# The product of an expert's two projections: one VectorE instruction from the PSUM bank, in place of a ScalarE copy and a GpSimd product

## The chip, the core and the metric

The kernel runs on one core of a Trainium2 chip. The metric is the device time of one execution in microseconds (us). The engines are TensorE (PE in the profile; its weight loads are PEld), VectorE (DVE), ScalarE (ACT), GpSimd (POOL) and SyncE (SP, which only issues DMAs). All data is float32.

## The reference, cut to what matters

Input x is (4, 1024, 256). It is normalised, and then goes both through a Mamba block and through a mixture of experts; the output is the sum of x and both.

```python
xn = _layernorm(x)
# Mamba block on xn: skip, x_in = two projections; conv over 4 taps, silu; delta = softplus(x @ wd1.T @ wd2.T + b)
h = exp(d_l * A) * h + (d_l * x_l) * b_l      # scan over 1024 positions, 512 channels x 16 states
y = (sum over states of h * c + x * W_D) * silu(skip);  out = resid + y @ out_w.T
# mixture of experts on xn: 8 experts, 2 for each token
h = einsum('td,edf->etf', xf, W1);  v = einsum('td,edf->etf', xf, V1)
out = einsum('etf,efd->etd', silu(h) * v, W2)   # each token weighted by its two scores
```

The change is in `silu(h) * v`.

## The kernel before, in words

The Mamba block works on chunks of 256 positions, 16 chunks (c = 0 to 15), 16 states in each (n). One step is u = 16 c + n. In each step POOL makes `ub` (products), PE transposes it into the banks `bps`, ACT makes `aexp`, DVE runs four scans `hb` (L1058) from `bps`, PE transposes `hb` into the banks `hps`, and DVE adds them up in `yac` (L1072, "the sum"). All other work is cut into pieces, which the tables `B_PLACES`, `O_PLACES` and `F_PLACES` put at 32 places of a chunk, two for each state. Every engine goes through the same list of places and does its own share of each piece, in this order: on PE `turn_products(u)`, the pieces of the even place, `turn_states(u - 1)`, the pieces of the odd place; on DVE `scans(u)`, the even place, `sum_states(u - 1)`, the odd place. Engines run their own instructions in order and wait for each other by semaphores.

Experts run in chunks 2 to 13. There are 72 tiles (j) of 128 dispatched tokens, six for each chunk, each in three pieces:

- FA(j): PE multiplies the tile by W1 into bank H (L941), ACT takes tanh (`th`), DVE makes `g1` (L1236) from `th` and bank H, which is 2 h times the sigmoid of h. PE also transposes `vs`, the product of tile j - 1, into bank G (L948).
- FB(j): PE multiplies by V1 into bank V (L963). ACT copies bank V to `vs` (L665), and POOL multiplies `vs` by `g1` in place (L775).
- FC(j + 1): PE multiplies the transposed product of tile j by W2 into bank X (L971).

The FB pieces stand at places 1, 10, 14, 20, 22 and 28 of a chunk, the FA pieces at 0, 8, 13, 16, 22 and 27.

Other pieces named below: O1, O2 and O3 finish the chunk before (O1 and O2 at place 2; in O2 DVE makes `tqO`, L1207, from bank G, which PE needs free for B1, L838, at place 5). B1 to B5 and others prepare the next chunk: X2 (DVE L1186, `x`, from two SBUF tiles, places 10 and 15), B4 at place 21 (PE writes banks H and V), SP at place 23 (two large activations on ACT, each with a table load beside it), B5 at place 29 (PE transposes `xc` into banks H and V, L882).

The banks H, V, X and G are each one PSUM bank, shared by all pieces. Two semaphores count for each: `full` (PE has written it) and `free` (the reader has done with it). `USES` holds the number of each piece's use of a bank:

```python
def wait_free(eng, b, piece):       # before a piece writes bank b
    at_least(eng, free[b], USES[b, piece])
def wait_taken(eng, b, piece):      # until this piece's use of bank b was read
    at_least(eng, free[b], USES[b, piece] + 1)
```

A semaphore `s_g` counts POOL's products; PE waits for it before it transposes `vs`, DVE before it writes `g1` again.

Of the kernel before, what the change touches and what calls it, by code (L numbers as in the profile page):

```python
# [18 lines left out]
ALU = mybir.AluOpType  # L19
ACT = mybir.ActivationFunctionType  # L20
# [175 lines left out]
def mamba_moe(nc, x, norm_w, skip_wT, in_wT, conv_w, conv_b, wd1T, wd2T, wd2_b, wBCT, A_log, W_D, out_wT,  # L196
# [3 lines left out]
    with ctx:  # L200
# [3 lines left out]
        def sem(name):  # L204
            return ctx.enter_context(nc.semaphore(name))
# [125 lines left out]
        s_th = sem("s_th")  # L331
        s_g = sem("s_g")
        y_out = [sem("y_out0"), sem("y_out1")]
# [160 lines left out]
        def _(act):  # L494
# [29 lines left out]
            def do(piece):  # L524
# [130 lines left out]
                elif kind == "FB":  # L655
                    j = piece[1]
                    if j + 1 < JT:
                        wait_full(act, "X", piece)
                        if j < 0:
                            act.wait_ge(lgt, TT)  # L660
                        nc.scalar.activation(xT[:, (j + 1) % 2, :, :], bank["X"][:, 0:D].rearrange("p (k t) -> p k t", k=KD),  # L661
                                             ACT.Copy).then_inc(free["X"], 1)
                    if j >= 0:
                        wait_full(act, "V", piece)
                        nc.scalar.activation(vs[:, :], bank["V"][:, :], ACT.Copy).then_inc(free["V"], 1)  # L665
                elif kind == "FC" and piece[1] > 0:
# [29 lines left out]
        def _(pool):  # L696
# [27 lines left out]
            def do(piece):  # L724
# [36 lines left out]
                elif kind == "D":  # L761
# [3 lines left out]
                    for t in (2 * piece[1], 2 * piece[1] + 1):  # L765
                        pool.wait_ge(xn_r, TT + t + 1)
                        for sl in (sl1, sl2):
                            nc.gpsimd.indirect_dma_start(
                                out=xbuf, out_offset=bass.IndirectOffsetOnAxis(ap=sl[:, t:t + 1], axis=0),
                                in_=ring[t % RING], in_offset=None).then_inc(disp[t % RING], 16)  # L770
                elif kind == "FB" and piece[1] >= 0:
                    j = piece[1]
                    wait_taken(pool, "V", piece)
                    wait_taken(pool, "H", ("FA", j))
                    nc.gpsimd.tensor_tensor(vs[:, :], g1[:, :], vs[:, :], ALU.mult).then_inc(s_g, 1)  # L775
                elif kind == "S":
                    t = piece[1]
                    if t == 0:
                        for k in range(2):
                            pool.wait_ge(y_out[k], 16 * JT // 2)  # L780
                    for tn in ahead(t):
                        gather(tn)
                elif kind == "LD":
                    gather(TT - 1)
# [22 lines left out]
        def _(pe):  # L807
# [22 lines left out]
            def do(piece):  # L830
# [100 lines left out]
                elif kind == "FA":  # L931
# [12 lines left out]
                    if j > 0:  # L944
                        wait_free(pe, "G", piece)
                        pe.wait_ge(s_g, j)
                        for k in range(FF // P):
# [47 lines left out]
        def _(dve):  # L995
# [170 lines left out]
            def do(piece):  # L1166
# [65 lines left out]
                elif kind == "FA" and piece[1] < JT:  # L1232
                    j = piece[1]
                    dve.wait_ge(s_th, j + 1)
                    at_least(dve, s_g, j)
                    v.scalar_tensor_tensor(out=g1[:, :], in0=th[:, :], scalar=1.0, in1=bank["H"][:, :],  # L1236
                                           op0=ALU.add, op1=ALU.mult).then_inc(free["H"], 1)
                elif kind == "S":
                    t = piece[1]
# [66 lines left out]
```

## Time and profile before

| | |
|---|---|
| device time, three runs | 1483.13 us median, 1481.66 to 1486.64 |
| profiled execution, span from first to last instruction | 1480.3 us |
| its own time beside the span | not recorded apart; the span is 1.4 us under the fastest run |
| busy: PE, DVE, ACT, POOL | 1279.1, 1243.6, 915.7, 868.9 us |
| share of the span | 86%, 84%, 62%, 59% |
| the chain that ended last | PE 65%, DVE 21%, issue 6%, ACT 3%, POOL 2% |

A share of busy time is an average over stages that differ: the router and the dispatch come up to about 260 us, the experts from there to about 1260 us, then the gathering of their results. In the rows of the trace, `x8` is a run of eight like instructions shown as one, whose first number is the start and whose second is the time from its start to its end. In square brackets stands the engine's idle time just before the run, and what ended it. The timeline counts two instructions for each of the 512 columns wide matmuls (x4 for the two of a piece).

### The profile page before, as it was taken

The numbers are of one execution on the slowest core, as the hardware profiler recorded it, in microseconds if no ns is written. First come the engines' busy times: TensorE is split into PE (matmuls) and PEld (weight loads), VectorE is DVE, ScalarE is ACT, GpSimd is POOL, SyncE is SP. The second block draws the span as 40 slices with busy tenths as digits, with TensorE's granted clock in tenths as the row PEclk, the third lists the DMA queues.
The fourth block names the chain that finished last, engine by engine and source line by source line (L and its number), as shares of the span: only waits on it lengthen the run. The fifth ranks groups of instructions, "written<-read, shape, count | busy, mean of one in ns | idle before, by whom it ended". The sixth has DMA issues, their size and how long they took to land.

```text
span 1480.3 us, 24598 instructions
## 1 busy us (share of the span) xinstructions
PE 1279.1 (86%) x7476; PEld 1028.4 (69%) x7476; DVE 1243.6 (84%) x2066; ACT 915.7 (62%) x2017; POOL 868.9 (59%) x1284
## 2 busy tenths in 40 slices
PE   4686674999999999999999999999999999865765
PEld 3575553777778777777778777777878777754654
DVE  6787876889797888889797888889797898999996
ACT  3776676576675757566675757566575756755330
POOL 0332477766668585766758585666758545335563
PEclk8797877999999999999999999999999999976876
DMA  9400826000000000001000000001000100144232
GB/s 316 144 2 0 291 97 211 17 25 24 29 23 30 29 23 22 29 23 30 26 26 30 30 22 23 26 26 30 23 29 30 30 23 15 49 133 133 74 112 84
DMA packets 76093, 86.43 MB, mean 58 GB/s; under 512 B 9920, under 2 KB 67136, under 8 KB 75968
## 3 DMA queue, kind: packets, MB, share of 16 engines
q1 hardware_dynamic: 69536, 68.02, 14.4%
q0 software_dynamic: 6144, 16.79, 3.8%
q8 instruction: 65, 1.06, 0.3%
q14 instruction: 60, 0.49, 0.1%
q10 hardware_dynamic: 288, 0.07, 0.0%
HBM read 49.46 MB, written 35.39 MB: 57 GB/s over the span
## 4 chain that ended last, share of the span: by engine, by line
PE 65%; DVE 21%; issue 6%; ACT 3%; POOL 2%; DMA 1%; DVEq 0%; POOLq 0%; SPq 0%; ACTq 0%
PE bps L818 12%; PE hps L827 11%; DVE hb L1058 9%; PE bankH L941 8%; PE bankX L971 8%; PE bankV L963 8%; PE bankG L850 3%; DVE yac L1072 3%; PE bankG L948 2%; PE bankG L860 2%; PE bankV L903 2%; PE bankG L863 2%; PE bankH L903 2%; PE bankV L850 1%; DVE tok L1255 1%
## 5 line engine op out<-in xcount | busy, mean ns | idle before, releaser
L1058 DVE TENSOR_TENSOR_SCAN hb<-aexp,carry,bps 128x256 f32<-128x256 f32 x768 | 509.8, 726 | 89.8 <-PE bps L818 71.5
L515 ACT ACTIVATE aexp<-delta,Am 128x256 f32<-128x256 f32 x1024 | 440.0, 503 | 60.9 <-DVE hb L1058 54.9
L1072 DVE SCALAR_TENSOR_TENSOR yac<-hps,BC,yac 128x512 f32<-128x512 f32 x480 | 334.7, 738 | 27.6 <-PE hps L827 27.4
L818 PE MATMUL bps<-idn,ub 128*128 128x128 f32 x2048 | 298.4, 290 | 62.7 <-DVE hb L1058 44.7
L827 PE MATMUL hps<-idn,hb 128*128 128x128 f32 x2048 | 292.1, 288 | 49.2 <-DVE yac L1072 44.7
L827 PEld LDWEIGHTS hps<-idn,hb 128*128 128x128 f32 x2048 | 250.6, 149 | 101.1 <-issue 79.0
L713 POOL TENSOR_SCALAR ub<-uT,BC 128x512 f32<-128x512 f32 x448 | 312.6, 710 | 11.8 <-ACT uT L602 10.5
L818 PEld LDWEIGHTS bps<-idn,ub 128*128 128x128 f32 x2048 | 250.3, 149 | 99.4 <-issue 59.5
L799 POOL COPY carry<-hb 128x4 f32<-128x4 f32 x256 | 55.7, 218 | 232.8 <-DVE hb L1058 231.2
L1058 DVE TENSOR_TENSOR_SCAN hb<-aexp,bps 128x256 f32<-128x256 f32 x256 | 154.6, 666 | 41.6 <-PE bps L818 37.9
L775 POOL TENSOR_TENSOR vs<-g,vs 128x512 f32<-128x512 f32 x72 | 91.9, 1276 | 166.2 <-ACT vs L665 165.3
L941 PE MATMUL bankH<-w,xT 128*128 x288 | 137.7, 600 | 2.9 <-issue 2.9
L971 PE MATMUL bankX<-w,gT 128*128 x576 | 136.2, 379 | 0.3 <-ACT xT L661 0.3
L963 PE MATMUL bankV<-v,xT 128*128 x288 | 135.5, 593 | 0.0
L971 PEld LDWEIGHTS bankX<-w,gT 128*128 128x128 f32 x576 | 106.5, 190 | 13.6 <-issue 0.7
L941 PEld LDWEIGHTS bankH<-w,xT 128*128 128x128 f32 x288 | 50.2, 191 | 41.8 <-issue 40.2
L665 ACT ACTIVATE vs<-bankV 128x512 f32<-128x512 f32 x72 | 42.9, 596 | 50.6 <-PE bankV L963 50.5
L376 POOL TENSOR_TENSOR y<-y,tqO 128x512 f32<-128x512 f32 x29 | 37.0, 1275 | 61.6 <-DVE tqO L1207 55.6
L963 PEld LDWEIGHTS bankV<-v,xT 128*128 128x128 f32 x288 | 49.1, 190 | 34.4 <-issue 34.4
L850 PE MATMUL bankG<-rnT,skw 128*128 128x256 f32 x256 | 63.8, 393 | 4.8 <-DVE tqO L1207 4.7
L649 ACT ACTIVATE th<-bankH 128x512 f32<-128x512 f32 x72 | 42.8, 595 | 39.6 <-PE bankH L941 39.6
L738 POOL TENSOR_SCALAR tap<-xin,cw 128x256 f32<-128x256 f32 x132 | 62.0, 478 | 4.3
(172 smaller groups left out, 1812.2 us busy)
## 6 DMA issues: line engine op xcount, KB each, us to landing
xbuf<-gT SPq DMA_DIRECT2D x8, 1152.0 KB, 11.0
tok<-xbuf SPq DMA_DIRECT2D x72, 128.0 KB, 2.2
ybuf<-tok SPq DMA_DIRECT2D x72, 128.0 KB, 1.7
w<-in_W SPq DMA_DIRECT2D x2, 4096.0 KB, 24.0
xch<-in_x SPq DMA_DIRECT2D x16, 256.0 KB, 2.9
w<-in_x SPq DMA_DIRECT2D x4, 1024.0 KB, 11.1
v<-in_V SPq DMA_DIRECT2D x1, 4096.0 KB, 15.9
tok<-in_x SPq DMA_DIRECT2D x32, 128.0 KB, 2.2
```

The source lines that it names most:

```text
L515: nc.scalar.activation(aexp[:, u % 2, e, :], delta[:, c % 2, e, :], ACT.Exp, scale=Am[:, e, n:n + 1]).then_inc(s_a, 1)
L713: nc.gpsimd.tensor_scalar(ub[:, u % 2, s, :], uT[:, c % 2, s, :], BC[:, c % 2, s, n:n + 1], 1.0, ALU.mult, ALU.mult).then_inc(s_ub, 1)
L738: return nc.gpsimd.tensor_scalar(dst, xin[:, e, w:w + CH], cw[:, e, w:w + 1], add, ALU.mult, ALU.mult if w else ALU.add)
L775: nc.gpsimd.tensor_tensor(vs[:, :], g1[:, :], vs[:, :], ALU.mult).then_inc(s_g, 1)
L818: mm = pe.transpose(bps[q][:, i * CH + s * P:i * CH + (s + 1) * P], ub[:, u % 2, s, e * P:(e + 1) * P], idn[:, :])
L827: mm = pe.transpose(hps[s][:, e * P:(e + 1) * P], hb[:, u % 2, e, s * P:(s + 1) * P], idn[:, :])
L850: mm = pe.matmul(bank[b][:, i * CH:(i + 1) * CH], w[:, k, e * P:(e + 1) * P], rnT[:, c % 2, k, :], start=(k == 0), stop=(k == KD - 1))
L941: mm = pe.matmul(bank["H"][:, :], xT[:, j % 2, k, :], w1[:, bass.ds(col + k * FF, FF)], start=(k == 0), stop=(k == KD - 1))
L963: mm = pe.matmul(bank["V"][:, :], xT[:, j % 2, k, :], v1[:, bass.ds(columns[j] + k * FF, FF)], start=(k == 0), stop=(k == KD - 1))
L971: mm = pe.matmul(bank["X"][:, 0:D], gT[:, k * P:(k + 1) * P], w2[:, bass.ds(columns[j] + k * D, D)], start=(k == 0), stop=(k == FF // P - 1))
L1058: v.tensor_tensor_scan(hb[:, u % 2, e, :], aexp[:, u % 2, e, :], bps[e // 2][:, (e % 2) * CH:(e % 2 + 1) * CH], first, ALU.mult, ALU.add). ...
L1072: ins = v.scalar_tensor_tensor(out=yac[:, c % 2, s, :], in0=hps[s][:, :], scalar=scale, in1=yac[:, c % 2, s, :], op0=ALU.mult, op1=ALU.add)
```

## The change

ACT's copy of bank V and POOL's product go. DVE multiplies `g1` by bank V and writes `vs`, in the same piece FB, and its end frees bank V. The semaphore `s_g` goes: PE's transposes of `vs` and DVE's next `g1` wait for the freeing of bank V instead.

```diff
@@ ScalarE, piece FB
-                    if j >= 0:
-                        wait_full(act, "V", piece)
-                        nc.scalar.activation(vs[:, :], bank["V"][:, :], ACT.Copy).then_inc(free["V"], 1)
@@ GpSimd
-                elif kind == "FB" and piece[1] >= 0:
-                    j = piece[1]
-                    wait_taken(pool, "V", piece)
-                    wait_taken(pool, "H", ("FA", j))
-                    nc.gpsimd.tensor_tensor(vs[:, :], g1[:, :], vs[:, :], ALU.mult).then_inc(s_g, 1)
@@ TensorE, piece FA
                         wait_free(pe, "G", piece)
-                        pe.wait_ge(s_g, j)
+                        wait_taken(pe, "V", ("FB", j - 1))
@@ VectorE
                     dve.wait_ge(s_th, j + 1)
-                    at_least(dve, s_g, j)
+                    if j > 0:
+                        wait_taken(dve, "V", ("FB", j - 1))
                     v.scalar_tensor_tensor(out=g1[:, :], in0=th[:, :], scalar=1.0, in1=bank["H"][:, :],
                                            op0=ALU.add, op1=ALU.mult).then_inc(free["H"], 1)
+                elif kind == "FB" and piece[1] >= 0:
+                    j = piece[1]
+                    wait_full(dve, "V", piece)
+                    wait_taken(dve, "H", ("FA", j))
+                    v.tensor_tensor(vs[:, :], g1[:, :], bank["V"][:, :], ALU.mult).then_inc(free["V"], 1)
```

DVE before, from the scans of place 24 to place 0 of the next chunk (`hb` are the scans, `yac` the sums, `g` is g1):

```order
L1058 SCALAR_TENSOR_TENSOR hb<-aexp,carry,bps 128x256 x4
L1072 SCALAR_TENSOR_TENSOR yac<-hps,BC,yac 128x512 x2
L1236 SCALAR_TENSOR_TENSOR g<-th,bankH 128x512
L1058 SCALAR_TENSOR_TENSOR hb<-aexp,carry,bps 128x256 x4
L1072 SCALAR_TENSOR_TENSOR yac<-hps,BC,yac 128x512 x2
L1058 SCALAR_TENSOR_TENSOR hb<-aexp,carry,bps 128x256 x4
```

DVE now, the same place:

```order
L1049 SCALAR_TENSOR_TENSOR hb<-aexp,carry,bps 128x256 x4
L1063 SCALAR_TENSOR_TENSOR yac<-hps,BC,yac 128x512 x2
L1228 SCALAR_TENSOR_TENSOR g<-th,bankH 128x512
L1049 SCALAR_TENSOR_TENSOR hb<-aexp,carry,bps 128x256 x4
L1234 TENSOR_TENSOR vs<-g,bankV 128x512
L1063 SCALAR_TENSOR_TENSOR yac<-hps,BC,yac 128x512 x2
```

The product (L1234) stands between the scans of place 28 and the sum. PE before, from FA at place 27 to B5 at place 29, with the semaphores that each row waits for:

```order
L948 MATMUL bankG<-idn,vs 128x128 [waits s_g,free_G]
...
L963 REGISTER_ALU [waits free_V]
L963 MATMUL bankV<-v,xT 128x512
...
L827 MATMUL hps<-idn,hb 128x128 [waits s_acc,s_scan]
...
L882 MATMUL bankH<-idn,xc 128x128 [waits free_H,uu]
...
L882 MATMUL bankV<-idn,xc 128x128 [waits free_V]
```

PE now, the same rows:

```order
L939 MATMUL bankG<-idn,vs 128x128 [waits free_V,free_G]
...
L954 REGISTER_ALU [waits free_V]
L954 MATMUL bankV<-v,xT 128x512
...
L818 MATMUL hps<-idn,hb 128x128 [waits s_acc,s_scan]
...
L873 MATMUL bankH<-idn,xc 128x128 [waits free_H,uu]
...
L873 MATMUL bankV<-idn,xc 128x128 [waits free_V]
```

PE's instructions stay in their order. The transposes of `vs` wait for `free_V` in place of `s_g`, and the `free_V` that B5 waits for is now given by DVE.

## Rows read from the trace of the kernel before

**Rows 1.** Busy time of each engine, experts' stretch of 1000 us, all windows together

```profile
sum 1000.00, PE 973.66 PEld 775.60 DVE 845.79 ACT 652.94 POOL 654.48; mean PE 81.14 PEld 64.63 DVE 70.48 ACT 54.41 POOL 54.54
```

**Rows 2.** Waits, 262 to 1262 us: total, times, longest

```profile
POOL vs L775 <- ACT vs L665: 165.3, 50, 6.6
...
PE bankG L838 <- DVE tqO L1207: 18.5, 12, 1.6
```

**Rows 3.** Groups of PE, 262 to 1262 us: busy, mean ns | idle before

```profile
L948 PE MATMUL bankG<-idn,vs 128*128 128x128 f32 x284 | 42.6, 273 | 0.0
```

**Rows 4.** Timeline, the start of chunk 6

```profile
607.14 0.66 DVE L1207 SCALAR_TENSOR_TENSOR tqO<-tqO,bankG 128x512 f32<-128x512 f32 x1
...
607.86 0.66 PE L838 MATMUL bankG<-idn,xch 128*128 128x128 f32 x4 [1.60 <-DVE tqO L1207]
```

**Rows 5.** Groups of DVE by form, and g1's own line (minimum/median/maximum)

```profile
L1144 DVE TENSOR_TENSOR v<-v,bankH 128x256 f32<-128x256 f32 x1 | 0.4, 420 | 0.0
...
L1236 DVE SCALAR_TENSOR_TENSOR g<-th,bankH x72: 652/686/690, 261.0 to 1257.1; 128x512 f32<-128x512 f32 x72
```

**Rows 6.** One line of DVE: duration ns minimum/median/maximum

```profile
L1186 DVE SCALAR_TENSOR_TENSOR x<-tqB,xc x32: 667/693/1217, 24.1 to 1318.3; 128x512 f32<-128x512 f32 x32
```

**Rows 7.** Timeline, places 27 to 30 of chunk 6

```profile
668.63 0.68 DVE L1236 SCALAR_TENSOR_TENSOR g<-th,bankH 128x512 f32<-128x512 f32 x1
...
669.23 2.66 DVE L1058 TENSOR_TENSOR_SCAN hb<-aexp,carry,bps 128x256 f32<-128x256 f32 x4
...
671.80 1.38 DVE L1072 SCALAR_TENSOR_TENSOR yac<-hps,BC,yac 128x512 f32<-128x512 f32 x2
671.82 0.60 PE L882 MATMUL bankV<-idn,xc 128*128 128x128 f32 x4
...
672.25 1.04 PE L818 MATMUL bps<-idn,ub 128*128 128x128 f32 x8
```

**Rows 8.** Timeline, places 12 to 22 of chunk 6

```profile
627.07 2.66 DVE L1058 TENSOR_TENSOR_SCAN hb<-aexp,carry,bps 128x256 f32<-128x256 f32 x4 [2.10 <-PE bps L818]
...
637.23 1.27 POOL L775 TENSOR_TENSOR vs<-g,vs 128x512 f32<-128x512 f32 x1
...
637.85 1.20 DVE L1186 SCALAR_TENSOR_TENSOR x<-tqB,xc 128x512 f32<-128x512 f32 x1 [0.94 <-ACT tqB L560]
...
650.17 1.39 DVE L1072 SCALAR_TENSOR_TENSOR yac<-hps,BC,yac 128x512 f32<-128x512 f32 x2
...
651.06 1.03 PE L873 MATMUL bankV<-dtT,wd 128*128 128x256 f32 x4
...
654.39 2.66 DVE L1058 TENSOR_TENSOR_SCAN hb<-aexp,carry,bps 128x256 f32<-128x256 f32 x4 [2.83 <-PE bps L818]
```

**Rows 9.** Timeline, places 22 to 26 of chunk 6

```profile
658.82 0.60 ACT L665 ACTIVATE vs<-bankV 128x512 f32<-128x512 f32 x1 [1.01 <-PE bankV L963]
659.26 1.41 DVE L1072 SCALAR_TENSOR_TENSOR yac<-hps,BC,yac 128x512 f32<-128x512 f32 x2 [1.50 <-PE hps L827]
...
663.16 1.38 DVE L1072 SCALAR_TENSOR_TENSOR yac<-hps,BC,yac 128x512 f32<-128x512 f32 x2
664.02 1.22 PE L827 MATMUL hps<-idn,hb 128*128 128x128 f32 x8
664.05 1.71 ACT L515 ACTIVATE aexp<-delta,Am 128x256 f32<-128x256 f32 x4
664.75 2.66 DVE L1058 TENSOR_TENSOR_SCAN hb<-aexp,carry,bps 128x256 f32<-128x256 f32 x4 [0.22 <-PE hps L827]
```

**Rows 10.** Timeline, places 1 and 2 of chunk 7

```profile
681.93 0.60 ACT L665 ACTIVATE vs<-bankV 128x512 f32<-128x512 f32 x1 [1.34 <-PE bankV L963]
...
682.47 2.66 DVE L1058 TENSOR_TENSOR_SCAN hb<-aexp,carry,bps 128x256 f32<-128x256 f32 x4 [0.94 <-PE bps L818]
```

**Rows 11.** Timeline, places 26 to 29 of chunk 12

```profile
1167.11 2.42 DVE L1058 TENSOR_TENSOR_SCAN hb<-aexp,bps 128x256 f32<-128x256 f32 x4 [0.46 <-ACT aexp L515]
...
1173.67 1.38 DVE L1072 SCALAR_TENSOR_TENSOR yac<-hps,BC,yac 128x512 f32<-128x512 f32 x2
...
1173.93 0.60 PE L882 MATMUL bankV<-idn,xc 128*128 128x128 f32 x4
```

More of the change, by code:

```diff
@@ L331, in mamba_moe @@
         s_th = sem("s_th")
-        s_g = sem("s_g")
         y_out = [sem("y_out0"), sem("y_out1")]
```

## The prediction, made before the changed kernel was run

> **What bounds the kernel now.** I read the busy times by stage, then the waits, then the timeline of one chunk, PE and DVE side by side. The product stands only in chunks 2 to 13, from 262 to 1262 us. In these 1000 us PE is busy for 973.66, DVE for 845.79, ACT and POOL for some 650 each [rows 1]. So PE is the bound there: a chunk repeats every 83.9 us, and at most 26 us in all are PE's idle time. Of these, 18.5 are the twelve times (1.6 us at most each) that PE waits for DVE's tqO at the start of a chunk [rows 2]. The long wait in the list, POOL's 165.3 us for ACT's copy of V, is a wait of an idle engine. The four transposes that consume the product, bankG from vs, were never late: no idle time before them [rows 3]. So a shorter way to vs buys nothing. What decides is (1) where DVE, which gets the work, has no slack against PE, and (2) when bank V comes free.
>
> The start of a chunk is such a place: tqO ends at 607.80, and PE goes on at 607.86 after 1.60 us of idle time [rows 4]. The hand-over from DVE to PE costs 0.06. DVE has no gap from its scans at place 2 up to there, so each delay of those scans is PE's.
>
> **Price of the new instruction.** No tensor_tensor of this width with one operand in PSUM stands in the trace. The nearest row is g1, 128x512 from bank H and an SBUF tile: 677 ns mean. At 128x256, a tensor_tensor from bank H takes 420 ns [rows 5]; it is half as wide, and so a floor. The ceiling is the longest x2 product, 1217 ns [rows 6]. I take 0.69 until the result is there, as g1 in the timeline, and 0.60 for the instruction behind it: from g1's start at 668.63 to that of the scans at 669.23 [rows 7]. That is 72 x 0.60 = 43 us more for DVE. ACT loses 72 copies of 0.60 us, POOL 72 products. Neither was bound, except as told under place 22.
>
> **Where it is covered.** There are six FB pieces in a chunk, at places 1, 10, 14, 20, 22 and 28. At place 10 the product delays a sum, and DVE then still has the idle 2.10 us before the scans of 627.07. At place 14 the idle 0.94 before x2 at 637.85 takes it. At place 20 it starts at about 650.17, where the sum stood, and 2.83 us of idle time follow at 654.39 [rows 8]. Bank V is also needed there by the next matmuls of PE, at 651.06: 650.17 + 0.69 + 0.06 = 650.92, in time by 0.14. These three cost nothing. If the cover failed, each would cost up to 0.60 x 12 = 7 us.
>
> **Place 22.** V is full at 658.82, when ACT's copy started. The product starts there, and the sum that stood at 659.26 moves to 659.42, by 0.16. From here DVE is what PE waits for: the transposes of 664.02 last 1.22 because the sum of 663.16 is still emptying their banks. They go with it, +0.16 for PE. The scans of 664.75 stood idle for 0.22. The view names PE, but the exponentials of ACT, started at 664.05, fit better [rows 9]. They sit behind a chain (copy of V, two large activations, two table loads) which begins earlier without the copy. So these scans start where DVE is ready, at 664.75 - 0.22 + 0.16 = 664.69, that is 0.06 earlier.
>
> **Place 28, the largest term.** B5 at place 29 writes bank V again. Before, ACT had emptied it. Now the product stands behind the scans of 669.23 in DVE's queue. It starts at 671.80 - 0.06 = 671.74, ends at 672.43, and PE can go on at 672.49, where before it went on at 671.82 [rows 7]: PE is now 0.67 late in all (0.16 of it already had). Behind it on DVE, the sum and the scans of the next state come 0.56 late, less than PE, so no more is added.
>
> **Place 1 of the next chunk.** V is full at 681.93 + 0.67 = 682.60; the product delays the scans to 683.20, where 682.47 stood with 0.94 us of idle time [rows 10]. So DVE enters the chain that ends at tqO 0.73 us late, and PE with it. After that chain DVE waits for PE again, and the next chunk begins afresh.
>
> **Chunks 4, 8 and 12** have shorter scans. In chunk 12 the wait for ACT was 0.46, so DVE gains 0.30 where the other chunks gain 0.06; the product at place 28 starts at about 1173.37, and V is free at 1174.12 against 1173.93 [rows 11]: 0.19, and 0.06 at place 1, make 0.25.
>
> **Sum.** 9 x 0.73 + 3 x 0.25 = 7.3 us. On the span of 1480.3 that gives 1487.6. The span is 2.8 below the median of the runs, 1483.13 (no separate time of the profiled execution is given), so I forecast 1490.4, 0.5% slower.
>
> **A rule against the trace.** When the x2 product of 637.85 took 1.20 us, POOL's product of two SBUF tiles was running; the shortest took 0.67 [rows 6, 8]. g1, with an operand in PSUM, took 652 to 690 ns in all 72 cases, whatever POOL did [rows 5]. So the new product should not be slowed by POOL. The Trainium skill (SBUF — State Buffer, Who interferes with whom) says that a DVE instruction with two SBUF inputs contends with a GpSimd instruction that reads SBUF, and one with at most one SBUF input does not. By that rule, the two trace observations agree, and 0.69 holds. The same skill (Perfetto Trace Analysis, Optimizing Scalar/DVE Operations) gives DVE about 65 ns more overhead on PSUM than on SBUF; an estimate from that page would add 0.065 at the three uncovered places, 12 x 3 x 0.065 = 2.3 us. g1's measured time already includes whatever PSUM costs, so I add nothing.
>
> **Rivals.**
> - *No change.* The wait for bank V is absent or hidden, and the remaining 0.16 + 0.06 per chunk make 2.6 us: 1485.8 or a little less. For it: all terms are tenths of a microsecond, read from modelled ends of matmuls. Against it: only one instruction lies between the scans' end and the need of V. Chance 0.22.
> - *DVE is the bound.* If the cover at places 10, 14 and 20 fails in part, up to 3 x 7 us come on top: 1491 to 1512; if every product counts in full, 43 us: 1526. Against it: DVE would be busy for 889 of 1000 us, with idle stretches of up to 2.8 us. Chance 0.10. The Trainium skill (Perfetto Trace Analysis, the same section) says that when DVE is saturated, work should go to Scalar; by that rule this change goes the wrong way, and the 43 us are its price.
> - *The product is slow.* If DVE and POOL block each other here as well, the product takes 1.22. That adds 0.53 at three places: 12 x 1.6 = 19 us, 1510. g1's 72 rows speak against it. Chance 0.03.
> - *Faster.* POOL's product no longer holds up the x2 product at place 15: 1.20 becomes 0.69, and 12 x 0.5 = 6 us come off DVE's chain: 1477. It decides only if PE waits for DVE just behind it. The waits show nearly none outside of the chunk's start (26 us of idle time, 18.5 of them for tqO), and the product of place 14 puts the 0.6 us back. Chance 0.07.
> - *The forecast*, 3 to 13 us slower, 1486 to 1496: chance 0.58.
>
> **How the numbers follow.** About 0.3%, 4.5 us, is what a measurement can tell from no change here. A tenth of the forecast's cases lie under it. Slower: 0.52 + 0.10 + 0.03 = 0.65, less a little for a mild case of the second rival: 0.64. Same: 0.06 + 0.22 less the part of it that is faster, 0.27. Faster: 0.09. The range takes the forecast and the no-change case, and cuts the long upper tail: 1482 to 1499. The forecast's own range is 1486 to 1496.
>
> **What the profile after would show.** Product: 72 rows on DVE, 0.65 to 0.70 us. PE's transposes of B5 into bank V: some 0.5 us idle before them, released by DVE's product, in nine of twelve chunks; PE idle for tqO still about 1.6. The period of a chunk: 84.6 in place of 83.9. ACT's chain before the exponentials at place 26: over half a microsecond earlier against the copy's start. x2 at place 15 under 1.2. What would make it wrong: no idle time before B5's transposes (no change), scans or sums that PE waits for between places 10 and 21 (more than forecast), or a product well over 0.7 us.

## The result and the profile after

The changed kernel took 1490.14 us (median of 12 runs, 1486.34 to 1494.57), the kernel before 1484.37 in the 12 runs beside it (1480.02 to 1487.65). The ratio is 1.004 with a 95% interval of [1.0027, 1.0054], so the change costs 5.8 us by the medians, and 4.0 to 8.0 by the interval. 1490.4 had been forecast, so the sum came out right. Its parts did not all come out, and the experiments below show which. Four of the timed runs below took 1750 to 7169 us (two with the register load moved in the changed kernel, one of the last experiment, one of the kernel before); all medians and ratios leave them out.

The span of the changed kernel's profile is 1484.4 us. From the waits of its experts' stretch (total, times, longest):

```profile
PE bankG L829 <- DVE tqO L1198: 18.5, 12, 1.6
```

PE's long wait is what it was, twelve waits of at most 1.6 us [rows 2]. The product itself has 72 rows, minimum, median and maximum 650, 676 and 690 ns. The x2 product is shown below it; its slowest row is now 901 ns where it was 1217 [rows 6]:

```profile
L1234 DVE TENSOR_TENSOR vs<-g,bankV x72: 650/676/690, 259.8 to 1263.2; 128x512 f32<-128x512 f32 x72
L1177 DVE SCALAR_TENSOR_TENSOR x<-tqB,xc x32: 667/693/901, 24.5 to 1321.9; 128x512 f32<-128x512 f32 x32
```

The groups of lines, again with busy time, mean ns and the idle time before:

```profile
L939 PE MATMUL bankG<-idn,vs 128*128 128x128 f32 x284 | 42.6, 273 | 0.0
L873 PE MATMUL bankV<-idn,xc 128*128 128x128 f32 x48 | 7.7, 283 | 1.7 <-DVE vs L1234 1.5
```

PE still never waits for the finished product (L939, as L948 in [rows 3]). The new entry is the second one: B5 waits for DVE's product to leave bank V, seven times, at most 0.3 us, in all for 1.5 us. Over twelve chunks that is far less than the forecast's half a microsecond each. The busy times of the experts' stretch, 262 to 1266 us (columns: length; then PE, PEld, DVE, ACT, POOL with their instructions; granted clock, DMA share, GB/s):

```profile
262.00:1266.00 1004.00, 975.00 (x5789) 773.90 (x5788) 879.98 (x1394) 613.63 (x1389) 561.18 (x924) 1.00 0.08 25
```

DVE has 34 us more, ACT 39 less, POOL 93 less than in [rows 1], and PE about the same in a stretch 4 us longer.

**The period.** The start of B1 (the transposes into bank G that wait 1.60 us for tqO [rows 4]) is a clean mark, once in each chunk. In the changed kernel the marks of chunks 6, 7 and 13 and the one behind chunk 13 are:

```profile
605.31 0.66 PE L829 MATMUL bankG<-idn,xch 128*128 128x128 f32 x4 [1.60 <-DVE tqO L1198]
...
689.77 0.66 PE L829 MATMUL bankG<-idn,xch 128*128 128x128 f32 x4 [1.60 <-DVE tqO L1198]
...
1194.17 0.66 PE L829 MATMUL bankG<-idn,xch 128*128 128x128 f32 x4 [1.60 <-DVE tqO L1198]
...
1282.22 0.66 PE L829 MATMUL bankG<-idn,xch 128*128 128x128 f32 x4 [1.60 <-DVE tqO L1198]
```

Chunk 6 is 689.77 - 605.31 = 84.46 us long, chunk 13 is 88.05. All twelve, as differences of such starts; chunk c runs from the B1 in it to the B1 of the next:

| chunk | 2 | 3 | 4 | 5 | 6 | 7 | 8 | 9 | 10 | 11 | 12 | 13 | sum |
|---|---|---|---|---|---|---|---|---|---|---|---|---|---|
| before | 83.91 | 83.46 | 83.52 | 83.94 | 83.93 | 83.50 | 83.54 | 83.97 | 83.98 | 83.46 | 83.50 | 84.85 | 1005.56 |
| after | 83.39 | 83.98 | 83.73 | 84.47 | 84.46 | 83.99 | 83.72 | 84.47 | 84.46 | 83.99 | 83.77 | 88.05 | 1012.48 |
| difference | -0.52 | +0.52 | +0.21 | +0.53 | +0.53 | +0.49 | +0.18 | +0.50 | +0.48 | +0.53 | +0.27 | +3.20 | +6.92 |

There are three things in this table: 0.5 us in each ordinary chunk and 0.2 in a chunk with short scans (0.73 and 0.25 forecast), a gain in chunk 2, and 3.2 us in chunk 13 that no step of the forecast had. Ahead of the first mark the profiled execution after was 3.3 us quicker (269.74 against 273.03), behind the last one 0.5 slower. Of the experts' work only the first tile's FA and FB stand ahead of it and the last tile's FC behind. The ten profiles up to the experiment on chunk 13 have the first mark anywhere from 269.74 to 274.67, in kernels that hardly differ up to there, so the 3.3 us are most likely spread between executions. They are why the two spans differ by only 4.1 us, while the runs' medians differ by 5.8.

**One ordinary chunk.** DVE and PE from place 26 of chunk 6 to place 1 of the next:

```profile
662.04 2.65 DVE L1049 TENSOR_TENSOR_SCAN hb<-aexp,carry,bps 128x256 f32<-128x256 f32 x4
...
669.08 0.66 DVE L1234 TENSOR_TENSOR vs<-g,bankV 128x512 f32<-128x512 f32 x1
669.79 0.66 PE L873 MATMUL bankV<-idn,xc 128*128 128x128 f32 x4 [0.23 <-DVE vs L1234]
...
671.02 2.66 DVE L1049 TENSOR_TENSOR_SCAN hb<-aexp,carry,bps 128x256 f32<-128x256 f32 x4
...
674.63 1.93 PE L932 MATMUL bankH<-w,xT 128*128 x4
...
679.85 0.69 DVE L1234 TENSOR_TENSOR vs<-g,bankV 128x512 f32<-128x512 f32 x1 [0.40 <-PE bankV L954]
680.45 2.65 DVE L1049 TENSOR_TENSOR_SCAN hb<-aexp,carry,bps 128x256 f32<-128x256 f32 x4
```

To set the two kernels side by side I measure from the chunk's B1 mark. That was 607.86 before [rows 4] and is 605.31 now, 2.55 us. B5's second half, into bank V, stood at 671.82 [rows 7], which would be 669.27 now; it stands at 669.79, 0.52 late. The product in front of it takes 0.66 and follows the scans without a gap; bank V is the obvious cause. But the idle time before B5 is only 0.23, and the matmul of FA at 674.63 is late as well, which B5 does not hold up directly. The next chunk's product stands at 679.85 with the scans 0.60 behind it, as forecast for place 1.

### The profile page after: what moved, and what is told of

It is laid out like the page before. It is cut to its first block, busy times and chain, and to the rows that moved or that the text cites. A ratio compares the mean times of both kernels' runs of the same rounds, so it can differ in the third digit from the quotient of the medians.

```text
span 1484.4 us, 24537 instructions
## 1 busy us (share of the span) xinstructions
PE 1280.7 (86%) x7476; PEld 1026.6 (69%) x7476; DVE 1280.1 (86%) x2138; ACT 877.4 (59%) x1945; POOL 776.9 (52%) x1212
## 3 DMA queue, kind: packets, MB, share of 16 engines
q8 instruction: 65, 1.06, 0.3%
## 4 chain that ended last, share of the span: by engine, by line
PE 61%; DVE 22%; issue 8%; ACT 5%; POOL 3%; DMA 2%; DVEq 0%; SPq 0%; ACTq 0%; POOLq 0%
PE bps L809 11%; PE hps L818 10%; DVE hb L1049 9%; PE bankH L932 8%; PE bankX L962 8%; PE bankV L954 7%; PE bankG L841 3%; DVE yac L1063 3%; PE bankG L939 2%; POOL xbuf L764 2%; PE bankG L851 2%; ACT aexp L514 2%; PE bankV L894 2%; PE bankG L854 1%; PE bankV L841 1%
## 5 line engine op out<-in xcount | busy, mean ns | idle before, releaser
L790 POOL COPY carry<-hb 128x4 f32<-128x4 f32 x256 | 50.8, 199 | 404.9 <-DVE hb L1049 402.8
L1228 DVE SCALAR_TENSOR_TENSOR g<-th,bankH 128x512 f32<-128x512 f32 x72 | 49.1, 681 | 19.6 <-ACT th L648 19.0
L610 ACT ACTIVATE tqO<-bankG 128x512 f32<-128x512 f32 x31 | 18.5, 598 | 80.2 <-PE bankG L841 80.2
```

The costliest lines, as they stand in the source:

```text
L790: nc.gpsimd.tensor_copy(carry[:, n, :], hb[:, u % 2, :, CH - 1]).then_inc(s_cc, 1)
```

## The experiments

Chunk 6 stands for the ordinary chunks in all of them. Single runs of one kernel spread over some 8 us, so they say little at this size; the periods say more, for they repeat: chunks 5, 6, 9 and 10 lie within 0.05 us of each other in the kernel before, and within 0.01 in the changed one (the widest are 0.17 with B5 in bank G and 0.15 with place 22 alone, so in those two a tenth of a microsecond says little). The medians of the kernel before were 1482.15 (7 runs) beside the first four kernels, 1483.73 (25 runs) beside the next four, and 1492.64 (20 runs) beside the last four. Those ran on another chip, where the first B1 stands at 280 to 282 us and not at 270 to 275; they are read by ratio and period.

**Which of the six places costs.** Three kernels make the product on DVE at some places and with ACT's copy and POOL's product at the others:

```
def by_pool(j):                      # False: DVE makes it
    return j % 6 in BY_POOL
BY_POOL = (0, 1, 2, 3, 4)            # e_dve28: place 28 on DVE alone
BY_POOL = (0, 1, 2, 3, 5)            # e_dve22: place 22
BY_POOL = (0, 4, 5)                  # e_dve_covered: places 10, 14, 20
```

*Place 28 alone.*

> Only the products of place 28 (12 of 72) are made by VectorE from bank V; the other 60 go by ScalarE's copy and GpSimd as before. My account: at place 28 the product stands behind the scans and holds bank V until B5 needs it, so the period of an ordinary chunk (start of B1 to start of B1) goes from 83.94 to 84.4 or 84.5, nearly all of the 0.53 that the whole change costs, and TensorE is idle before B5's transposes into bank V, released by VectorE's product. Rival, VectorE's load spread evenly: a sixth of 0.53, 84.03.

1489.64 us in one run; the period of chunk 6 is 84.57, just above the 84.4 to 84.5 expected. Twelve of the 72 products cost all that the 72 cost (+0.64 against +0.53), so a load spread over all places is refuted. The wait in the list of the experts' stretch, and then DVE and PE at place 29 (the lines of this kernel are numbered otherwise: L1260 is the product, L899 is B5):

```profile
PE bankV L899 <- DVE vs L1260: 5.6, 11, 0.8
```

```profile
672.14 0.66 DVE L1260 TENSOR_TENSOR vs<-g,bankV 128x512 f32<-128x512 f32 x1
...
672.85 0.66 PE L899 MATMUL bankV<-idn,xc 128*128 128x128 f32 x4 [0.54 <-DVE vs L1260]
```

Here the idle time is the half microsecond that the prediction named: without the product of place 22, B5's first half comes in time, and its second half waits visibly. In the full change the first half is itself later, and the product earlier, so the wait shows as 0.23.

These rows also say why place 28 costs more alone (0.64) than all six together (0.53). The B1 mark of this kernel is at 608.21, so the product starts 63.93 behind it, and B5's second half stands at 64.64, 0.68 late against the kernel before (63.96): almost exactly the 0.67 forecast. In the full change the product starts at 669.08 - 605.31 = 63.77, 0.16 sooner. There ACT has no copy at place 22, its exponentials come earlier, and DVE's scans with them; that takes 0.16 back at place 28. The places don't add up: with place 28 on DVE, the other five together are a gain in the ordinary chunks.

*Place 22 alone.*

> Only the products of place 22 are made by VectorE. My account: the sum behind it and TensorE with it are 0.16 later, and the scans of place 26 start 0.14 earlier as ScalarE's chain lacks the copy; the period of an ordinary chunk becomes 84.05 to 84.1. Rival, load spread evenly: 84.03. Second rival, ScalarE's missing copy is a gain in itself: under 83.9. The relative place of the scans at place 26 tells my account from the rivals.

1482.75 us in one run; the period is 84.05, +0.12 (+0.1 to 0.15 expected). The sums and scans behind the product:

```profile
660.93 1.38 DVE L1089 SCALAR_TENSOR_TENSOR yac<-hps,BC,yac 128x512 f32<-128x512 f32 x2
...
662.23 2.65 DVE L1075 TENSOR_TENSOR_SCAN hb<-aexp,carry,bps 128x256 f32<-128x256 f32 x4
```

Sums to scans is 1.30 us. It was 664.75 - 663.16 = 1.59 with 0.22 of idle time [rows 9]. So the idle time is gone. ACT's exponentials start at 660.05 here and at 659.87 in the full change, 54.64 and 54.56 behind the B1 marks, where they stood 56.19 behind: 1.6 us earlier, the copy's 0.6 and the 1.01 of idle time in front of it [rows 9]. PE's transposes into `hps`, which the view names as the releaser, come later and not earlier (56.39 against 56.16 behind the marks), which leaves the exponentials as what the scans had waited for, as the prediction supposed. DVE takes back 0.07 more of the 0.16 than I had counted.

*The three covered places.*

> The products of places 10, 14 and 20 (36 of 72) are made by VectorE, the other 36 as before. My account: they are covered, so the period of an ordinary chunk stays at 83.94 to within 0.05, with the idle time of VectorE before the scans of place 12 and of place 22 shorter by 0.6; only chunk 13, where VectorE also makes the next chunk's convolution, is longer, by 1 to 3 us. Rival, load spread evenly: half of 0.53, 84.2 in every ordinary chunk.

1484.82 us in one run. Ordinary chunks have 83.90 to 83.98 us, unchanged: covered, as forecast. Chunk 13 is 1.26 us longer, and chunk 2 is 1.09 shorter. The second looks like the fourth rival of the prediction (POOL's product no longer slows the x2 product), but most of it is another thing. Before, in chunk 2:

```profile
289.33 1.27 POOL L775 TENSOR_TENSOR vs<-g,vs 128x512 f32<-128x512 f32 x1
...
302.34 0.63 ACT L560 ACTIVATE tqB<-xc 128x512 f32<-128x512 f32 x1 [2.71 <-POOL xc L750]
...
303.00 1.21 DVE L1186 SCALAR_TENSOR_TENSOR x<-tqB,xc 128x512 f32<-128x512 f32 x1 [2.03 <-ACT tqB L560]
...
306.84 0.66 PE L818 MATMUL bps<-idn,ub 128*128 128x128 f32 x4 [0.54 <-DVE hb L1058]
```

and with the products of places 10, 14 and 20 on DVE (L1203 is x2):

```profile
300.90 0.64 ACT L577 ACTIVATE tqB<-xc 128x512 f32<-128x512 f32 x1 [2.43 <-POOL xc L767]
301.57 0.77 DVE L1203 SCALAR_TENSOR_TENSOR x<-tqB,xc 128x512 f32<-128x512 f32 x1 [0.25 <-ACT tqB L577]
```

The x2 product waited for `tqB` from ACT, ACT for the convolution `xc` from POOL, and in POOL's queue the product of place 10 (1.27 us, at 289.33) stood ahead of that convolution. PE waited 0.54 for the scans behind x2. Without POOL's products, `tqB` and x2 start 1.16 and 1.15 us sooner against the B1 marks of chunk 2 (273.03 and 272.75), and x2 takes 0.77 in place of 1.21. The shorter x2 is 0.44 us, less than half of the gain of 1.09; the earlier convolution covers it alone. In chunk 6 x2 waits 0.94 for its input and not 2.03 [rows 8], and PE does not wait behind it.

**How place 28 reaches PE.** The prediction says: by bank V. B5 has another bank to go to:

```
-    "B5": ["H", "V"]   ...  for s, b in enumerate("HV"):
+    "B5": ["H", "G"]   ...  for s, b in enumerate("HG"):
```

> The changed kernel, with the second half of B5 in bank G in place of bank V; all products on VectorE. My account: the wait for bank V at place 29 is gone, TensorE is 0.16 late from place 22 and VectorE some 0.2 to 0.3 at the end of a chunk, so the period of an ordinary chunk is 84.15 to 84.25 in place of 84.46, and the kernel 2 to 4 us faster than the changed one. Rival, VectorE's queue is the bound there with or without the bank: 84.46 stays.

1488.05 us (4 runs), ratio to before 1.0051 [1.0034, 1.0068]; the period is 84.40 (84.57 in chunk 5). This is a miss: the wait that I took for the carrier is gone, and the cost stays. B5's second half (now into bank G) no longer waits for DVE's product, and yet:

```profile
669.58 0.66 DVE L1234 TENSOR_TENSOR vs<-g,bankV 128x512 f32<-128x512 f32 x1
669.90 0.60 PE L873 MATMUL bankG<-idn,xc 128*128 128x128 f32 x4
...
671.48 2.65 DVE L1049 TENSOR_TENSOR_SCAN hb<-aexp,carry,bps 128x256 f32<-128x256 f32 x4
673.84 1.04 PE L809 MATMUL bps<-idn,ub 128*128 128x128 f32 x8
675.03 1.98 PE L932 MATMUL bankH<-w,xT 128*128 x4 [0.16 <-issue]
```

Between the transposes into bps, which end at 674.88, and FA's matmul there is a short idle time with the releaser "issue": PE waits for nothing in the profile. In the kernel before this matmul stands 0.9 us behind the end of the DVE work that PE waits for, at two places of the chunk (scans end 675.75, matmul 676.66; sum ends 664.54, matmul 665.44), and here too (674.13, 675.03). By the program, the scans (at place 27 the sum) are what PE's queue last waits for before FA. What stands between is a load into PE's registers, the column of the expert's weights, `te` (L936 of the kernel before; PEldq is the queue of the weight loads, the numbers are minimum, median, maximum):

```profile
L936 PEldq TENSOR_LOAD <-te x72: 296/301/489, 256.2 to 1253.0; - x72
L936 PEldq FUSED_REGOPS  x72: 151/151/165, 256.7 to 1253.5; - x72
```

My reading: it is a second way for a late DVE to reach PE. The wait holds back the load, and the load the matmul, while the transposes ahead of it run out. That can be tried by loading the next tile's column at the end of FB, ahead of the wait:

```
 FA:  -    col = pe.value_load(te[0:1, j:j + 1], min_val=0, max_val=(EXPERTS - 1) * WE)
      +    col = columns[j]          # (for j == 0 it is loaded here)
 FB:  +    if j + 1 < JT:
      +        columns[j + 1] = pe.value_load(te[0:1, j + 1:j + 2], min_val=0, max_val=(EXPERTS - 1) * WE)
```

*Both ways closed.*

> The changed kernel with B5's second half in bank G, and with TensorE's register load of the expert's column for tile j + 1 moved from the start of FA(j + 1) to the end of FB(j), ahead of the waits for VectorE. My new account: at the end of a chunk VectorE's lateness reaches TensorE by two ways side by side, the wait for bank V and the register load, which starts only when TensorE's wait for the last scan is over and costs 0.9 us; each alone holds TensorE back by the same 0.4 to 0.5, so only both removed show a gain. The period of an ordinary chunk is 84.0 to 84.1 in place of 84.46, the kernel some 4 to 5 us faster than the changed one. Rival, VectorE's queue is the bound without TensorE's waits: 84.4 or more stays.

1483.26 us, ratio 0.9994 [0.998, 1.0007]; the period is 83.98, as expected. The matmul now follows the transposes with no idle time:

```profile
674.31 1.04 PE L809 MATMUL bps<-idn,ub 128*128 128x128 f32 x8
675.18 1.88 PE L932 MATMUL bankH<-w,xT 128*128 x4
```

*The register load alone.*

> The changed kernel with only the register load moved; B5 stays in bank V. My new account: the matmuls of FA at place 27 start 0.4 earlier, but the wait of B5 for bank V then holds TensorE at the same time as before, so the period of an ordinary chunk stays at 84.4 to 84.46. If the register load alone was the way by which the cost came, it is 84.0 to 84.1.

1488.17 us, ratio 1.003 [1.002, 1.0041]; the period is 84.41, as expected. Now it is bank V that shows, with the wait that the prediction had in its text (L1236 is the product):

```profile
674.49 0.66 PE L873 MATMUL bankV<-idn,xc 128*128 128x128 f32 x4 [0.68 <-DVE vs L1236]
```

The four periods of chunk 6 side by side: 84.46 as changed, 84.40 without the wait for bank V, 84.41 without the register load behind the wait, 83.98 without both. Of the 0.48 us that the two edits give together, each alone gives at most 0.06: the two ways stand side by side and carry the same lateness. No single edit would have shown this. It does not follow that these 0.48 us are the cost of the change, for the register load costs in the kernel before too, as the next run shows.

*The register load in the kernel before.*

> The kernel before, with only the register load moved. My new account: both FA starts that follow a wait for VectorE (places 27 and 0) come 0.3 to 0.4 earlier, not added up, so the period of an ordinary chunk goes from 83.94 to about 83.55, and the kernel is 4 to 5 us faster than before, 0.3%. Rival, the idle time before these matmuls is covered by VectorE's chain at the start of the chunk: 83.9 stays.

1475.93 us (4 runs), ratio 0.9948 [0.9931, 0.9965]; the period is 83.56 (83.93 before, 83.55 expected). In the kernel before, the load was not covered either. It is faster than both kernels. FA's matmuls before and with the load moved:

```profile
L941 PE MATMUL bankH<-w,xT 128*128 x284 | 135.5, 600 | 2.9 <-issue 2.9
```

```profile
L941 PE MATMUL bankH<-w,xT 128*128 x284 | 133.6, 593 | 0.0
```

The idle time of 2.9 us and 1.9 us of busy time are gone; over the twelve chunks it gains 1005.56 - 1000.97 = 4.6.

Compared like with like, a third way is left. With the load moved, the kernel before has 83.56, the changed one 84.41, and the changed one without the wait for bank V 83.98. So bank V carries 0.43, and 0.42 of the cost is there with both ways closed (if B5's other bank costs the kernel before nothing, which was not tried). First the kernel before with the load moved (its B1 mark is at 603.56), then the changed one with both edits (606.29), the sum of place 28 and PE's transposes of `hb`:

```profile
667.56 1.38 DVE L1074 SCALAR_TENSOR_TENSOR yac<-hps,BC,yac 128x512 f32<-128x512 f32 x2
668.43 0.63 PE L827 MATMUL hps<-idn,hb 128*128 128x128 f32 x4
```

```profile
670.63 1.40 DVE L1065 SCALAR_TENSOR_TENSOR yac<-hps,BC,yac 128x512 f32<-128x512 f32 x2
671.52 0.63 PE L818 MATMUL hps<-idn,hb 128*128 128x128 f32 x4
```

Against the marks the sum is 0.34 late, since the product stands in front of it, and the transposes, which need the bank that the sum empties, are 0.36 late. The FA matmul is 0.35 late (672.10 against 675.18), and the next B1 0.42. This third way was read from the rows; no edit closed it.

**Chunk 13.** In this chunk DVE also makes the convolution of chunk 14 (DVE_CONV), in the changed kernel as before. PE in its places 10 to 18, in the changed kernel:

```profile
1214.03 1.22 PE L818 MATMUL hps<-idn,hb 128*128 128x128 f32 x8 [0.36 <-DVE yac L1063]
...
1230.37 0.63 PE L809 MATMUL bps<-idn,ub 128*128 128x128 f32 x4 [1.33 <-DVE hb L1049]
1231.56 0.66 PE L809 MATMUL bps<-idn,ub 128*128 128x128 f32 x4 [0.56 <-DVE hb L1049]
1232.05 3.51 PE L851 MATMUL bankG<-x,wd 128*128 128x256 f32 x8
```

and the same matmuls in the kernel before:

```profile
1213.17 1.22 PE L827 MATMUL hps<-idn,hb 128*128 128x128 f32 x8
...
1228.92 0.63 PE L818 MATMUL bps<-idn,ub 128*128 128x128 f32 x4 [1.32 <-DVE hb L1058]
1230.10 0.66 PE L818 MATMUL bps<-idn,ub 128*128 128x128 f32 x4 [0.56 <-DVE hb L1058]
1230.60 1.89 PE L860 MATMUL bankG<-x,wd 128*128 128x256 f32 x8
```

Against the B1 marks (1194.17 and 1193.74) the first row is 0.43 us late: DVE is behind with a sum, and the product of place 10 stands in front of it. The transposes into bps are 1.02 late: 1230.37 - 1194.17 = 36.20 against 35.18. So the two products cost 1.0 us here. The waits of 1.33 and 0.56 themselves are old: DVE was late with these scans before the change too. The third part is in the last row. Eight matmuls take 3.51 us where they took 1.89, 1.62 more. The stretch of the waits and the one behind it, in the changed kernel, and then in the kernel before, each moved to the same matmuls (columns as above):

```profile
1229.00:1232.00 3.00, 1.11 (x9) 0.87 (x9) 3.00 (x5) 2.74 (x6) 0.44 (x2) 1.00 0.11 37
1232.00:1235.30 3.30, 3.30 (x10) 2.64 (x9) 3.30 (x7) 0.04 (x1) 1.09 (x2) 0.52 0.03 5
```

```profile
1227.55:1230.55 3.00, 1.12 (x9) 0.87 (x9) 3.00 (x6) 3.00 (x8) 0.44 (x2) 1.00 0.22 66
1230.55:1233.85 3.30, 3.30 (x25) 3.09 (x23) 3.30 (x7) 0.09 (x1) 1.08 (x2) 1.00 0.02 5
```

PE was busy for 1.11 and 1.12 of 3.00 us, the same. Behind it the granted clock was 0.52 in the one, close to the 1.2 GHz level, and 1.00 in the other, the 2.4 GHz level. So 3.20 is 1.0 from the two products, 1.6 from the low clock, and the usual half microsecond at the chunk's end. The experiment gives the convolution of chunk 14 back to POOL, which takes DVE's lateness away and with it the waits:

```
-DVE_CONV = (0, 1, 2, 14, 15)
+DVE_CONV = (0, 1, 2, 15)
```

> The changed kernel with the convolution of chunk 14 made by GpSimd (as those of chunks 3 to 13) in place of VectorE; it is made during chunk 13. My account of chunk 13, whose period was 88.05 after the change and 84.85 before: VectorE was already full there with the convolution, so that the products of places 10 and 14 are not covered (0.44 and 0.60), and TensorE's longer wait brought a stretch at a granted clock of 0.72 (1.6 us). Without that convolution on VectorE the period of chunk 13 falls to 84.5 to 85.5, some 3 us off the kernel. Rival, the low clock comes for another reason and place: 86 or more stays.

1485.8 us, ratio 1.0013 [1.0001, 1.0024]. Chunk 13 has 82.76 us, below the 84.5 to 85.5 expected; chunk 6 has 84.54 (84.46 with it). The cause was right and its size too small, since not only the new cost goes but also the 1.9 us of waits that the kernel before had (84.85 there). PE is busy throughout, at full clock:

```profile
1229.00:1236.00 7.00, 7.00 (x54) 6.48 (x53) 6.12 (x11) 3.94 (x11) 2.61 (x5) 1.00 0.01 2
```

**Put together.** Three kernels ask what is left of the change once its costs are mended, and where the product is made best. All have the register load moved and 14 out of DVE_CONV; the first has the change and B5 in bank G, the second is the kernel before, the third (BY_POOL = (5,)) makes 60 products on DVE and those of place 28 as before.

> The changed kernel with all three: register load moved, B5's second half in bank G, convolution of chunk 14 on GpSimd. My account: the gains stand at different places and add up: ordinary chunks 83.99, chunk 13 some 82.5 to 83, and 10 to 11 us off the changed kernel, 1479, 0.3% under the kernel before.

1488.39 us, ratio 0.9975 [0.9957, 0.9992]; chunk 6 83.99, chunk 13 82.71, all experts 1001.85.

> The kernel before with the register load moved and the convolution of chunk 14 on GpSimd; the products stay with ScalarE and GpSimd. My account: VectorE gets no products, so this stays ahead of the changed kernel with the same two repairs by 0.4 us a chunk: ordinary chunks 83.56, chunk 13 82.3 to 84, in all 1472 to 1475. Rival: GpSimd, which has 12 products more than 1 us each in that kernel, is too slow for the convolution in chunk 13, and it takes 85 or more.

1485.45 us, ratio 0.9945 [0.9928, 0.9962]; chunk 6 83.59, chunk 13 82.39, experts 998.74. The rival, that chunk 13 would gain nothing here, falls. (The times expected in us were for the other chip.) In the ratio the 2.4 us of chunk 13 don't show against the register load alone (0.9948), but the two intervals are 3.4 thousandths wide each, and 2.4 us are 1.6.

> The changed kernel with only the products of place 28 given back to ScalarE and GpSimd (60 of 72 on VectorE), register load moved, convolution of chunk 14 on GpSimd; B5 in bank V. My account: what is left of the cost is place 22, some 0.1 us a chunk, so ordinary chunks take 83.6 to 83.75 and the kernel is within 2 us of the one before with the same repairs. Rival, the load on VectorE counts wherever it stands: 83.9.

1483.86 us (4 runs), ratio 0.9939 [0.9918, 0.996]; chunk 6 83.51, chunk 13 82.13, chunk 2 82.52, experts 997.59. The ordinary chunk is quicker than the 83.6 to 83.75 expected: nothing is left of place 22's cost there. Its ratio is the lowest, but the interval holds that of the kernel before with the same two edits. By the sum of its periods it is 1.15 us ahead of that one: 1.06 in chunk 2 (83.58 there), 0.26 in chunk 13 and 0.06 to 0.08 in each ordinary chunk, against 0.23 lost in each of the three short ones (83.27 and 83.04). So in sum the 60 products cost nothing. The twelve of place 28 cost 0.48 in an ordinary chunk (83.99 against 83.51) and nothing in a short one (83.27 in both), as far as B5's other bank costs nothing itself; that bank was not tried in the kernel before. Which product costs the 0.23 in the short chunks was not tested.

**Something earlier on PE to fill the tqO wait.** One edit was tried on the 1.6 us at the chunk's start, in the kernel before with the register load moved: B1 at place 6 in place of 5.

> The kernel before with the register load moved and B1 of the chunks that follow the common table at place 6 in place of 5 (ahead of it TensorE has the transposes of the next products to do, while VectorE finishes tqO). My account: the idle 1.60 us before B1 is VectorE's chain seen from TensorE; one piece of 0.87 us moves into it, so the period falls by 0.5 to 0.9, to 82.7 to 83.1. Rival: the next transposes wait for VectorE's scans just as long, and B2 behind B1 then waits for ScalarE: no gain or a loss.

1493.54 us, ratio 1.0009 [0.9999, 1.002], against 0.9948 without the edit. A miss: the period is 83.72 and not 82.7 to 83.1. PE has other work during tqO now, and waits behind it, first for the scans and then, at B1, for ACT, much as the rival said:

```profile
614.29 0.66 PE L818 MATMUL bps<-idn,ub 128*128 128x128 f32 x4 [0.40 <-DVE hb L1060]
615.42 0.84 PE L838 MATMUL bankG<-idn,xch 128*128 128x128 f32 x4 [0.47 <-ACT xch L531]
```

Chunk 13 has 86.21 us there, and a low clock behind the same pair of waits (1.31 and 0.56): L860, its eight matmuls as above, takes 3.53 us. The twelve periods make 1004.3 us, 3.35 more than without the edit; the rest of the difference in the ratio, some 6 us, is not explained by them.

## Why the prediction was right, and where it was not

**The bound and the price of the instruction** held. PE stays the bound with its 1.6 us for tqO, L939 has no idle time, and the product takes 673 ns in the mean against 690 taken, 0.60 to the start of what follows it.

**Covered places (10, 14, 20): nothing.** Right in eleven chunks; not in chunk 13, where DVE has a convolution of its own. I had costed the twelve chunks as nine ordinary and three short ones and had not looked at chunk 13 apart, though DVE_CONV names chunk 14, whose convolution is made there. The prediction's own words for this risk were those of the second rival, "if the cover at places 10, 14 and 20 fails in part". It failed in one chunk, for 1.0 us; the 1.6 of the low clock came on top.

**Place 22: +0.16, and the scans of place 26 0.06 earlier.** Measured alone 0.12 in the period. By the timeline of the full change DVE starts its product of place 28 at 669.08, where the sum stood before at 671.80 - 2.55 = 669.25: 0.17 earlier. The forecast had it 0.06 earlier, so the mechanism is right, the size a tenth off.

**Place 28, the largest term.** It is the right place: alone it costs 0.64, and B5's second half is then 0.68 late, for 0.67 forecast. PE is 0.52 late at bank V where 0.67 was given; the 0.11 us of the scans and a product of 0.66 in place of 0.69 make nearly all of that. What failed is the sentence "Behind it on DVE, the sum and the scans of the next state come 0.56 late, less than PE, so no more is added". It holds as a sum, since nothing was added. But it took bank V for the way that decides. The late scans reach PE too, through the wait ahead of FA and the register load behind it, by nearly the same amount, and with both ways closed 0.42 of the cost is still there, with PE 0.36 late behind the late sum. A reader who had acted on the prediction and moved B5 to another bank would have gained nothing (84.40 against 84.46).

**Place 1: +0.06.** Not measured apart, but the timeline of the full change has it. The product starts at 679.85, when PE has filled bank V, and the scans behind it stand at 680.45 - 605.31 = 75.14 against 682.47 - 607.86 = 74.61: 0.53 late, and so is the next B1. With place 28 alone, the scans are 0.63 late and the next B1 0.64. PE's transposes just before (into bps) are 0.47 late in the full change and 0.63 with place 28 alone, so the product of place 1 adds the 0.06. The chunk as a whole has 0.53 and not 0.73; the short ones 0.18 to 0.27, for a forecast of 0.25. The short scans stand in chunks 4, 8 and 12, and so do the three small differences of the table.

**The sum.** 7.3 us were forecast in the experts and 6.9 measured in the one profile; the medians differ by 5.8. That 1490.14 came so close to 1490.4 is also due to the kernel before, which had 1484.37 beside the changed one and not the 1483.13 that the forecast started from. For chunks 3 to 12 the forecast was 7 x 0.73 + 3 x 0.25 = 5.9, and they make 4.2; chunk 2 makes -0.52 and chunk 13 +3.20, each in place of 0.73. So the total was hit in part by luck: a cost that I had not seen stood in for terms that were too large, 0.51 in the mean of the seven ordinary chunks in place of 0.73.

**The rivals.** The first, no change (2.6 us slower at most), is refuted by the interval, which begins at 4.0. The second, DVE as the bound, is refuted as a uniform load, and right in one chunk. The slow product is refuted: its 72 rows end at 690 ns. The x2 product is faster as the fourth rival said (901 ns at most), but only chunk 2 gains, and more from POOL's earlier convolution than from that. The Trainium skill (SBUF — State Buffer, Who interferes with whom) let the product be free of POOL and the x2 product of two SBUF inputs not; both are seen here (the product took 690 ns at most; x2 took 1.21 us beside POOL's product and 0.77 without it). The 65 ns more on PSUM that the Trainium skill gives (Perfetto Trace Analysis, Optimizing Scalar/DVE Operations) can't show between product and g1, which both read a bank. The rows nearest to a comparison don't show it either: g1 took 652 ns at least and 686 in the median, x2, of two SBUF tiles, 667 and 693 [rows 5, 6].

**What stays open.** Why the clock falls in chunk 13 in some kernels and not in others. The pair of waits (1.3 and 0.56) stands there in the kernel before, in the changed one and in those of place 28, of place 22, of the covered places and of the last experiment. Behind it eight matmuls take 1.89 us in the first, the third and the fifth, and in the kernel before with the register load moved, and 3.2 to 3.5 us in the others, as in those with B5 in bank G, with the register load moved in the changed kernel, and with both. With place 28 alone, behind 1.31 and 0.56:

```profile
1235.35 1.89 PE L877 MATMUL bankG<-x,wd 128*128 128x256 f32 x8
```

Where the waits are gone, no profile shows the low clock. So 1.6 of the 5.8 us may belong to the moment at which the waits fall and not to the change; whether all timed runs of the changed kernel have it, one profile can't tell. In the short chunks place 28 alone costs 0.5 to 0.9 us, and the whole change 0.2; why was not followed up.

## What to carry to other kernels

Moving work to an engine with idle time is costed place by place, in each stage that differs and not only in the ordinary one: in sum 60 of 72 products were free here, those of place 28 cost half a microsecond in each ordinary chunk, and two cost another half microsecond each in the one chunk where the engine had a second job. When a late result is found, list every wait of the next engine that could carry the lateness before one is mended, since parallel waits hide each other, and test them in pairs. Then make the same edits in the old kernel: what they give there (0.37 us a chunk here) is no cost of the change. Look at what stands in a queue between a wait and the first real instruction: a register load there can be on the path. Moved, it gave 4.6 us in the experts' chunks, two thirds of what the change costs there.

## What was not expected of the hardware

A load of one number into TensorE's registers takes 0.30 us and the operations on it 0.15, and the matmul behind it started 0.9 us after the DVE work that ended the wait ahead of it. With the load moved, 0.58 of that is left (scans end 671.52, matmul 672.10 in the kernel before), in which PE runs the transposes. In the profile the load shows only as 0.16 to 0.36 us "issue" before FA. Moved ahead of the wait it gave 0.37 us in an ordinary chunk, a ratio of 0.9948 [0.9931, 0.9965]. And behind two waits of 1.9 us together TensorE ran eight matmuls at the 1.2 GHz level in some kernels (3.51 us) and at 2.4 GHz in others (1.89), with the same busy time in the 3 us ahead (1.11 and 1.12).
